# Handing the last gathered column of nine tiles from GpSimd to SyncE, fetched row by row

## The chip, the core and the metric

The kernel runs on one core of a Trainium2 chip. The metric is the device time of one execution in microseconds; the time given is the median of three runs. The change is judged against the time of the kernel before on the same chip.

## What is computed

A recommender's forward pass (DLRM) for 2048 samples, in float32. Each sample has 13 dense features and 26 indices, one into each of 26 tables of 12500 rows of 64 values (256 bytes a row).

```python
h = relu(dense @ dw1 + db1); dense_emb = relu(h @ dw2 + db2)      # (2048, 64)
sparse_emb = emb_tables[f_ids, sparse_idx]                        # (2048, 26, 64)
emb = concatenate([dense_emb[:, None, :], sparse_emb], axis=1)    # (2048, 27, 64)
inter = einsum('bfd,bgd->bfg', emb, emb)
pairs = inter[:, iu0, iu1]                                        # upper triangle, 351
z = concatenate([emb.reshape(2048, -1), pairs], axis=1)
z = relu(z @ ow1 + ob1); z = relu(z @ ow2 + ob2); z = relu(z @ ow3 + ob3)
return z @ ow4 + ob4
```

## The kernel before

The 2048 samples are 16 tiles of 128, a sample to a partition. Each engine has its own program, written out by hand; semaphores join them, and there is no scheduler.

**GpSimd (POOL)** fetches the rows. For each tile `t` it issues 26 indirect DMAs, one for each column `c` (table) of the indices: each brings 128 rows of 256 bytes into `emb[:, t % 4, c // 2, ...]`, 128 partitions at once (L261). The 26 columns are 13 pairs, and the pairs stand in four groups, `GROUPS = [(0, 4), (4, 8), (8, 12), (12, 13)]`: columns 0 to 7, 8 to 15, 16 to 23, and 24 and 25. Each group of each of the four ring places has a semaphore `gathered`. GpSimd's queue has gates (L242 to L260): at column 0, 4, 12, 16, 20 and 24 of a tile it waits until TensorE has got to a given step of this tile or the one before. The gate at column 4 of a tile is "all four groups of the tile before are transposed".

**TensorE (PE)** works through the tile in this order (L819 to L838): transposes of group 0 (L635), the second half of the pair products of the tile before (`gram`, L671), layer 1 of the first features (L683, L692), the pairs of the tile before (L654, L700), transposes of group 1, the turned hidden layer of the tile before (L707), more of layer 1, then transposes of group 2 and of group 3, the rest of layer 1 (ten instructions on the profile's row), and the first half of this tile's `gram`. For every fourth tile or so an upper layer (`upper`, L724, L729, L733) is set in: in tiles 4 to 11 one after the first half of `gram`, in tiles 13 and 14 also ahead of the transposes of group 2 and 3. The last tile, 15, has a finer order of its own (L839 to L869) and ends with the last layers and the store of its results.

**VectorE and ScalarE** evacuate what TensorE leaves in PSUM. VectorE first turns the indices into row numbers (L278, L280, L283), then sets constants, then waits for TensorE's first transposes of group 1.

**SyncE (SP)** issues the loads of weights (L221 to L229), and then only six stores of results `out_dram<-y` (L236), each one run of up to 512 values from one partition, after a wait for the last upper layer of the batch.

Of the kernel before, what the change touches and what calls it, by code (L numbers as in the profile page):

```python
# [6 lines left out]

F32 = mybir.dt.float32
I32 = mybir.dt.int32
U32 = mybir.dt.uint32  # L10
ALU = mybir.AluOpType
ACT = mybir.ActivationFunctionType

P = 128

GROUPS = [(0, 4), (4, 8), (8, 12), (12, 13)]
BATCHES = [(0, 4), (4, 8), (8, 12), (12, 14), (14, 15), (15, 16)]
LAST = BATCHES[-1][0]
LAST_GROUPS = [(0, 4), (4, 8), (8, 10), (10, 12), (12, 13)]


def bass_dlrm_kernel(
    nc: bass.Bass,
    dense_t: bass.AP,
    idx: bass.AP,
    first: bass.AP,
    table: bass.AP,
    dw1: bass.AP,
    dw2: bass.AP,
# [11 lines left out]
    D = dw1.shape[1]  # L41
    H1, H2, H3 = ow1.shape[1], ow2.shape[1], ow3.shape[1]
    TILES = B // P
    NF = idx.shape[2]
    NP = NF // 2
# [8 lines left out]
    RING = 4  # L54
    NG = len(GROUPS)
# [7 lines left out]
    with ExitStack() as ctx:  # L63
        def sb(name, shape, dt=F32):
            return ctx.enter_context(nc.sbuf_tensor(name, shape, dt))

        def psum(name, shape):
            return ctx.enter_context(nc.psum_tensor(name, shape, F32))

        def sem(name):  # L70
            return ctx.enter_context(nc.semaphore(name))

        tr_ps = psum("tr_ps", [P, 2, CHUNK])
        gram_ps = psum("gram_ps", [P, SETS, CHUNK])
        l1_ps = [psum(f"l1_ps{i}", [P, CHUNK]) for i in range(2)]

        first_sb = sb("first_sb", [P, 2, NF], I32)
        idx_raw = sb("idx_raw", [P, TILES, NF], I32)
        wrap = sb("wrap", [P, TILES, NF])
        idx_f = sb("idx_f", [P, TILES, NF])  # L80
        rows = sb("rows", [P, TILES, NF], U32)
        emb = sb("emb", [P, RING, NP, 2 * D])

        feat = [sb(f"feat{i}", [P, NP, P]) for i in range(2)]
        slots = [sb(f"slots{i}", [P, HALF, SETS, QUAD]) for i in range(2)]
# [33 lines left out]
        gathered = [[sem(f"gathered{r}_{n}") for n in range(NG)] for r in range(RING)]  # L119
# [45 lines left out]
        last_l4 = sem("last_l4")  # L165
        last_y = sem("last_y")

        w1_dram = ow1[D:D + NP * P, :].rearrange("(k p) n -> p k n", p=P)

        block = ctx.enter_context(nc.Block())  # L170

        def end_stage(t):

            if 4 <= t < 12:
                return divmod(t - 4, 4)
            return {12: (2, 0), 13: (2, 2), 14: (3, 2)}.get(t)
# [5 lines left out]
        def groups(t):  # L182
            return LAST_GROUPS if t == LAST else GROUPS

        def out_count(stage):
            return 4 * stage[0] + stage[1] + 1
# [25 lines left out]
        def last_turned(c):  # L212

            return (tr_ps[0:PR, 0, 0:P], tr_ps[0:PR, 1, 0:P], l1_ps[0][0:PR, 0:P])[c]

        def upper_cols(b):
            return (BATCHES[b][1] - BATCHES[b][0]) * P

        @block.sync
        def _(sp):  # L220
            sp.dma_start(first_sb[:], first).then_inc(first_in, 16)  # L221
            sp.dma_start(ident_sb[:], ident).then_inc(ident_in, 16)
            sp.dma_start(w1d_sb[:], ow1[0:D, :]).then_inc(w1d_in, 16)
            for n, (a, b) in enumerate(GROUPS):
                sp.dma_start(w1_sb[:, a:b, :], w1_dram[:, a:b, :]).then_inc(w1_in[n], 16)
            sp.dma_start(w1p_sb[:], ow1_pairs.rearrange("(c r) n -> r c n", r=PR)).then_inc(w1p_in, 16)
            sp.dma_start(w2_sb[:], ow2.rearrange("(k p) n -> p k n", p=P)).then_inc(w234_in, 16)
            sp.dma_start(w3_sb[:], ow3.rearrange("(k p) n -> p k n", p=P)).then_inc(w234_in, 16)
            sp.dma_start(w4_sb[:], ow4).then_inc(w234_in, 16)  # L229

            for b, (a, e) in enumerate(BATCHES):
                if a == LAST:
                    sp.wait_ge(last_y, 1)
                else:
                    sp.wait_ge(upper_out, 4 * b + 4)
                sp.dma_start(out[a * P:e * P, :].rearrange("b o -> o b"), y[:, a * P:e * P]).then_inc(out_stored, 16)  # L236
            sp.wait_ge(out_stored, 16 * len(BATCHES))

        @block.gpsimd
        def _(pool):  # L240
            for t in range(TILES):
                pool.wait_ge(rows_in, min(t, 1) + 1)  # L242
                for n, (a, b) in enumerate(GROUPS):
                    if t >= 1:
                        if n == 0:
                            pool.wait_ge(transposed, t * NG - 2)
                            if t >= 2:
                                pool.wait_ge(h1_turned, t - 1)
                        elif n == 2:
                            pool.wait_ge(transposed, t * NG + 1)  # L250
                            pool.wait_ge(gram_done, 2 * t)
                        elif n == 3:
                            pool.wait_ge(transposed, t * NG + 2)
                    for c in range(2 * a, 2 * b):
                        if t >= 1 and c == 4:
                            pool.wait_ge(transposed, t * NG)
                        elif t >= 1 and c == 12:
                            pool.wait_ge(gram_done, 2 * t - 1)
                        elif t >= 1 and c == 20:
                            pool.wait_ge(pairs_turned, t)  # L260
                        pool.indirect_dma_start(  # L261
                            out=emb[:, t % RING, c // 2, c % 2 * D:(c % 2 + 1) * D], out_offset=None, in_=table,
                            in_offset=bass.IndirectOffsetOnAxis(ap=rows[:, t, c:c + 1], axis=0),
                        ).then_inc(last_gathered[(c // 2 - a) // 2] if t == LAST and n == 2 else gathered[t % RING][n], 16)

        @block.vector
        def _(dve):
            step = 0
            for a, b in ((0, 1), (1, TILES)):
                if a == 0:  # L270
                    dve.wait_ge(first_in, 16)
                    r = first_sb[:, 1:2, :]
                else:
                    dve.wait_ge(idx_in, 16)
                    r = idx_raw[:, a:b, :]
                w, f = wrap[:, a:b, :], idx_f[:, a:b, :]
                base = first_sb[:, 0:1, :].to_broadcast([P, b - a, NF])
# [3 lines left out]
                                               op0=ALU.max, op1=ALU.add).then_inc(idx_step, 1)  # L281
                dve.wait_ge(idx_step, step + 2)
                nc.vector.scalar_tensor_tensor(out=rows[:, a:b, :], in0=f, scalar=float(V - 1), in1=base,  # L283
                                               op0=ALU.min, op1=ALU.add).then_inc(rows_in, 1)
                step += 2
            for i in range(2):
                nc.vector.memset(slots[i][:, :, :, SLOTS:QUAD], 0.0).then_inc(consts_in, 1)
                nc.vector.memset(pairs_b[i][:, NPAIR:NPAIR + 1], 1.0).then_inc(consts_in, 1)
                nc.vector.memset(pairs_b[i][:, NPAIR + 1:PC * PR], 0.0).then_inc(consts_in, 1)
            dve.wait_ge(dense_w_in, 4 * 16)  # L290

            def evac_features(t, n):
# [52 lines left out]
            def last_group_slots(n):  # L345
                a, b = groups(LAST)[n]
                dve.wait_ge(transposed, LAST * NG + n + 1)
                src = tr_ps[0:D, n % 2, 0:(b - a) * P].rearrange("p (k c h j) -> p h j c k", k=b - a, h=2, j=HALF)
                for h in range(2):
                    last = nc.vector.tensor_copy(slots[LAST % 2][h * D:(h + 1) * D, :, :, a:b], src[:, h])  # L350
                last.then_inc(slots_dve, 1)
# [258 lines left out]
        def _(pe):  # L610
# [12 lines left out]
            def transposes(t, n):  # L623
                a, b = GROUPS[n]
                if n >= 2:
                    pe.wait_ge((slots_act, slots_dve)[n % 2], 2 * t + 1)
                if n == 1 and t >= 1 and end_stage(t - 1):
                    pe.wait_ge(upper_out, out_count(end_stage(t - 1)))
                if n == 2 and t >= 1:
                    pe.wait_ge(pairs_in, t)  # L630
                if n == 3 and mid_stages(t):
                    pe.wait_ge(upper_out, out_count(mid_stages(t)[0]))
                pe.wait_ge(gathered[t % RING][n], (t // RING + 1) * 32 * (b - a))
                for k in range(a, b):
                    last = nc.tensor.transpose(tr_ps[:, n % 2, (k - a) * P:(k - a + 1) * P], emb[:, t % RING, k, :],  # L635
                                               ident_sb[:])
                last.then_inc(transposed, 1)

            def last_transposes(n):
                a, b = LAST_GROUPS[n]  # L640
                if n in (2, 3):
                    pe.wait_ge(last_gathered[n - 2], 32 * (b - a))
                else:
                    pe.wait_ge(gathered[LAST % RING][3], (LAST // RING + 1) * 32)
                for k in range(a, b):
                    last = nc.tensor.transpose(tr_ps[:, n % 2, (k - a) * P:(k - a + 1) * P], emb[:, LAST % RING, k, :],
                                               ident_sb[:])
                last.then_inc(transposed, 1)
# [287 lines left out]
```

## Time and profile before

| | us |
|---|---|
| median of 3 runs (543.19 to 543.59) | 543.25 |
| the profiled execution | 543.07 |
| its span, first to last instruction | 541.3 |
| TensorE busy with matmuls | 442.5 (82%) |
| GpSimd busy | 392.8 (73%), 416 gathers |
| chain that ended last | POOL 48%, PE 24%, issue 18%, DMA 7% |

The span is what the trace shows; the rest, 1.8 us, lies around it. "Issue" in the chain is time in which an engine waited for nothing that the profile shows; between two gathers of GpSimd it is a constant part of their pitch. A row "idle before <- releaser" says how long the engine stood still ahead of the instruction and what ended that.

### The profile page before, as it was taken

What the parts mean: (1) busy time and instruction counts of PE and PEld (TensorE: products, weight loads), DVE (VectorE), ACT (ScalarE), POOL (GpSimd) and SP (SyncE); (2) the same over time, 40 slices, a digit from 0 to 9 for tenths busy, and PEclk for the clock granted to TensorE, in tenths of its full rate; (3) what the DMA queues carried; (4) which work ended last, traced back from release to release, by engine and by line L of the source; (5) the groups of instructions that cost most, each with busy time, mean ns of one, the idle gap of its engine ahead of it and who ended that gap; (6) DMA issues with size and microseconds to landing.
All of it is one profiled execution on the core that took longest, in us unless ns stands there. A gap on an engine that the chain in (4) does not pass through costs nothing.

```text
span 541.3 us, 5812 instructions
## 1 busy us (share of the span) xinstructions
PE 442.5 (82%) x2262; PEld 235.0 (43%) x2262; DVE 151.4 (28%) x295; ACT 149.0 (28%) x334; POOL 392.8 (73%) x420
## 2 busy tenths in 40 slices
PE   3997879586895969879596997979789598898997
PEld 1245335242533535345253543535344254535686
DVE  1021414132140331414132140432214133241342
ACT  1423124131321422224141231323124141422422
POOL 5777777777777777777777777777777777777750
PEclk9998979799797988989798897999979799999999
DMA  8633323233332333323233232323323233332320
GB/s 265 151 48 28 26 27 28 26 28 27 27 26 27 27 26 28 27 26 28 27 28 27 26 28 26 28 26 29 26 26 28 26 27 26 28 26 26 28 23 2
DMA packets 17168, 19.40 MB, mean 36 GB/s; under 512 B 7359, under 2 KB 8386, under 8 KB 17127
## 3 DMA queue, kind: packets, MB, share of 16 engines
q0 software_dynamic: 13312, 13.66, 30.3%
q1 hardware_dynamic: 3408, 5.02, 2.8%
q10 hardware_dynamic: 420, 0.34, 0.3%
q8 instruction: 18, 0.29, 0.2%
q14 instruction: 10, 0.08, 0.0%
HBM read 18.99 MB, written 0.01 MB: 35 GB/s over the span
## 4 chain that ended last, share of the span: by engine, by line
POOL 48%; PE 24%; issue 18%; DMA 7%; DVE 1%; ACT 1%; POOLq 0%
POOL emb L261 48%; DMA emb<-table_dram,rows 7%; PE l_ps L692 7%; PE gram_ps L671 6%; PE l_ps L700 3%; PE tr_ps L635 2%; PE tr_ps L724 1%; PE l_ps L786 1%; PE gram_ps L786 1%; PE l_ps L683 1%; DVE pairs L310 1%; PE l_ps L707 0%; PE tr_ps L654 0%; ACT h L486 0%; DMA first_sb<-first_dram 0%
## 5 line engine op out<-in xcount | busy, mean ns | idle before, releaser
L261 POOL DMA_INDIRECT emb<-table_dram,rows x416 | 392.6, 944 | 130.1 <-issue 121.0
L692 PE MATMUL l_ps<-w_sb,feat 128*128 128x512 f32 x390 | 200.9, 665 | 0.9 <-DVE feat L296 0.9
L692 PEld LDWEIGHTS l_ps<-w_sb,feat 128*128 128x128 f32 x390 | 80.5, 217 | 101.1 <-issue 98.2
L635 PE MATMUL tr_ps<-ident_sb,emb 128*128 128x128 f32 x203 | 39.7, 315 | 69.8 <-DMA emb<-table_dram,rows 68.5
L329 DVE COPY gram_c<-gram_ps 32x432 f32<-32x432 f32 x60 | 36.5, 609 | 145.5 <-PE gram_ps L671 145.1
L635 PEld LDWEIGHTS tr_ps<-ident_sb,emb 128*128 128x128 f32 x203 | 26.6, 155 | 103.6 <-issue 89.4
L296 DVE COPY feat<-tr_ps 128x512 f32<-128x512 f32 (+2 forms) x33 | 16.1, 489 | 177.6 <-PE tr_ps L635 174.8
L671 PEld LDWEIGHTS gram_ps<-slots 64*128 64x128 f32 x960 | 57.0, 191 | 14.5 <-issue 13.7
L671 PE MATMUL gram_ps<-slots 64*128 64x108 f32 x960 | 62.2, 281 | 0.3 <-DVE gram_c L329 0.3
L469 ACT COPY gram_c<-gram_ps 32x432 f32<-32x432 f32 x60 | 30.5, 508 | 114.1 <-PE gram_ps L671 113.4
L449 ACT COPY feat<-tr_ps 128x512 f32<-128x512 f32 (+1 forms) x32 | 18.5, 577 | 130.5 <-PE tr_ps L635 129.8
L700 PE MATMUL l_ps<-w1p_sb,pairs 118*128 118x512 f32 x90 | 42.6, 610 | 9.8 <-DVE pairs L310 9.8
L457 ACT COPY slots<-tr_ps 64x256 f32<-64x256 f32 (+1 forms) x128 | 50.3, 393 | 1.1
L305 DVE COPY slots<-tr_ps 64x256 f32<-64x256 f32 (+2 forms) x128 | 44.3, 346 | 1.3
L336 DVE STREAM_TRANSPOSE gram_b<-gram_c 128x864 f32<-128x864 f32 x15 | 28.1, 1871 | 0.8
L700 PEld LDWEIGHTS l_ps<-w1p_sb,pairs 118*128 118x128 f32 x90 | 15.9, 190 | 27.8 <-issue 15.3
L486 ACT ACTIVATE h<-l_ps 128x512 f32<-128x512 f32 x15 | 9.0, 597 | 64.1 <-PE l_ps L700 64.1
L724 PE MATMUL tr_ps<-h1t,w_sb 128*128 128x512 f32 x48 | 22.1, 604 | 0.0
L310 DVE COPY pairs<-tr_ps 118x384 f32<-118x384 f32 x15 | 8.4, 557 | 30.0 <-PE tr_ps L654 30.0
L683 PE MATMUL l_ps<-w1d_sb,dense_e 64*128 64x512 f32 x30 | 16.6, 635 | 0.0
L613 PE MATMUL gram_ps<-dense_sb,dw_sb 13*64 13x512 f32 x8 | 7.1, 1063 | 8.9 <-DMA dw_sb<-dw_dram 8.9
L724 PEld LDWEIGHTS tr_ps<-h1t,w_sb 128*128 128x128 f32 x48 | 8.7, 190 | 9.6 <-issue 9.1
(103 smaller groups left out, 197.1 us busy)
## 6 DMA issues: line engine op xcount, KB each, us to landing
emb<-table_dram,rows POOLq DMA_INDIRECT x416, 3.3
w_sb<-ow_dram SPq DMA_DIRECT2D x3, 1024.0 KB, 10.0
w1p_sb<-ow_pairs_dram SPq DMA_DIRECT2D x1, 708.0 KB
w_sb<-ow_dram SPq DMA_DIRECT2D x1, 512.0 KB, 20.9
w_sb<-ow_dram SPq DMA_DIRECT2D x1, 256.0 KB, 12.0
idx_raw<-idx_dram ACTq DMA_DIRECT2D x1, 208.0 KB, 2.6
w1d_sb<-ow_dram SPq DMA_DIRECT2D x1, 128.0 KB, 4.3
w_sb<-ow_dram SPq DMA_DIRECT2D x1, 128.0 KB, 6.4
```

The source lines that it names most:

```text
L261: pool.indirect_dma_start(out=emb[:, t % RING, c // 2, c % 2 * D:(c % 2 + 1) * D], out_offset=None, in_=table, in_offset=bass.IndirectOffs ...
L305: last = nc.vector.tensor_copy(slots[t % 2][h * D:(h + 1) * D, :, :, base:base + b - a], src[:, h])
L329: last = nc.vector.tensor_copy(dst, src)
L336: nc.vector.transpose(gram_b[t % 2][:, 0:SLOTS, :], gram_c[:].rearrange("p i g -> p g i")).then_inc(gram_turned, 1)
L457: last = nc.scalar.copy(slots[t % 2][h * D:(h + 1) * D, :, :, base:base + b - a], src[:, h])
L469: last = nc.scalar.copy(dst, src)
L635: last = nc.tensor.transpose(tr_ps[:, n % 2, (k - a) * P:(k - a + 1) * P], emb[:, t % RING, k, :], ident_sb[:])
L671: mm = nc.tensor.matmul(gram_ps[:, bank, r * GCOLS:(r + 1) * GCOLS], x.rearrange("p c f -> p (c f)"), x[:, :, 0:SLOTS], start=True, stop=True)
L683: nc.tensor.matmul(l1_ps[t % 2][:], dense_e[:, t * P:(t + 1) * P], w1d_sb[:], start=True, stop=False)
L692: nc.tensor.matmul(l1_ps[t % 2][:], feat[t % 2][:, n - 1, :], w1_sb[:, n - 1, :], start=False, stop=False)
L700: mm = nc.tensor.matmul(l1_ps[t % 2][:], pairs[t % 2][:, c, :], w1p_sb[:, c, :], start=False, stop=c == PC - 1)
L724: mm = nc.tensor.matmul(upper_ps(b, s)[:, 0:n], w2_sb[:, k, s * P:(s + 1) * P], h1t[b % 2][:, k, 0:n], start=(k == 0), stop=(k == M1 - 1))
```

## The change

For the nine tiles of `OWN` (2, 4, 5, 7, 8, 10, 12, 13, 14) column 25, the last, is no longer gathered by GpSimd. SyncE fetches its 128 rows one at a time: it loads 32 byte addresses at a time from SBUF into registers, and issues for each a DMA of 256 bytes into one partition of a buffer of its own (`own`, with a place for each of the nine tiles, so no place is used twice). Column 24 of these tiles, which shares the pair with column 25, is gathered by GpSimd into the same buffer. The byte addresses come from four VectorE instructions on one partition of 1152 values (9 x 128), fed by one more load on SyncE's queue. TensorE's group 3 waits in these tiles for one gather fewer and for all 128 fetches. The host only passes the same indices a second time, in another order.

```diff
+OWN = [2, 4, 5, 7, 8, 10, 12, 13, 14]
+HELD = 32
...
+        own = sb("own", [P, len(OWN), 2 * D])
+        own_raw = sb("own_raw", [1, 2, len(OWN) * P], I32)
+        own_f = sb("own_f", [1, 2, len(OWN) * P])
+        own_at = sb("own_at", [1, len(OWN) * P], U32)
...
+        def pair_of(t, k):
+            return own[:, OWN.index(t), :] if t in OWN and k == NP - 1 else emb[:, t % RING, k, :]
+
+        def landed(t, n):
+            a, b = GROUPS[n]
+            return 16 * sum(2 * (b - a) - (n == NG - 1 and s in OWN) for s in range(t % RING, t + 1, RING))
...
                 sp.dma_start(w1_sb[:, a:b, :], w1_dram[:, a:b, :]).then_inc(w1_in[n], 16)
+            sp.dma_start(own_raw[:], own_idx).then_inc(own_in, 16)
             sp.dma_start(w1p_sb[:], ow1_pairs.rearrange("(c r) n -> r c n", r=PR)).then_inc(w1p_in, 16)
...
+            sp.wait_ge(own_rows, 1)
+            held = [sp.alloc_register(f"row{j}") for j in range(HELD)]
+            flat = table.rearrange("r d -> (r d)").bitcast(U8)
+            for i in range(len(OWN)):
+                for q in range(P // HELD):
+                    sp.reg_load(held, own_at[0:1, i * P + q * HELD:i * P + (q + 1) * HELD])
+                    for j in range(HELD):
+                        at = sp.snap(held[j], min_val=0, max_val=(NF * V - 1) * D * 4)
+                        p = q * HELD + j
+                        sp.dma_start(own[p:p + 1, i, D:2 * D].bitcast(U8),
+                                     flat[bass.ds(at, 4 * D)].rearrange("(o d) -> o d", o=1)).then_inc(fetched[i], 16)
...
+                        if t in OWN and c == NF - 1:
+                            continue
                         pool.indirect_dma_start(
-                            out=emb[:, t % RING, c // 2, c % 2 * D:(c % 2 + 1) * D], out_offset=None, in_=table,
+                            out=pair_of(t, c // 2)[:, c % 2 * D:(c % 2 + 1) * D], out_offset=None, in_=table,
...
+            dve.wait_ge(own_in, 16)
+            r, base = own_raw[:, 0, :], own_raw[:, 1, :]
+            w, f = own_f[:, 0, :], own_f[:, 1, :]
+            nc.vector.tensor_scalar(w, r, 0.0, float(V), ALU.is_lt, ALU.mult).then_inc(own_step, 1)
...
+            nc.vector.tensor_scalar(own_at[:], w, float(4 * D), None, ALU.mult).then_inc(own_rows, 1)
             dve.wait_ge(dense_w_in, 4 * 16)
...
-                pe.wait_ge(gathered[t % RING][n], (t // RING + 1) * 32 * (b - a))
+                pe.wait_ge(gathered[t % RING][n], landed(t, n))
+                if t in OWN and n == NG - 1:
+                    pe.wait_ge(fetched[OWN.index(t)], 16 * P)
```

SyncE's program of the kernel before, from the last load of weights for layer 1 to the stores (`w_sb` stands for the weights of several layers):

```order
L226 DMA w1p_sb<-ow_pairs_dram 118x3x512
L227 DMA w_sb<-ow_dram 128x4x256
L228 DMA w_sb<-ow_dram 128x2x128
L229 DMA w_sb<-ow_dram 128x1
L236 DMA out_dram<-y 1x512 x3
```

The same place in the changed kernel. The last two rows come 36 times in all (9 tiles, 4 quarters of 32 rows) ahead of the first store:

```order
L246 DMA own_raw<-own_idx_dram 1x2304
L247 DMA w1p_sb<-ow_pairs_dram 118x3x512
L248 DMA w_sb<-ow_dram 128x4x256
L249 DMA w_sb<-ow_dram 128x2x128
L250 DMA w_sb<-ow_dram 128x1
L257 TENSOR_LOAD own_at
L261 DMA own<-table_dram 1x256 x32
```

One load has come in ahead of `w1p_sb`, and 36 register loads and 1152 fetches stand between the weights and all six stores. Each fetch is two instructions on SyncE: a register move (the copy that `snap` makes, which this listing leaves out) and the DMA.

GpSimd's program of the changed kernel from tile 0 on. The kernel before has in its place the one row `L261 DMA emb<-table_dram,rows 128x64 x416`:

```order
L296 DMA emb<-table_dram,rows 128x64 x76
L296 DMA own<-table_dram,rows 128x64
L296 DMA emb<-table_dram,rows 128x64 x50
L296 DMA own<-table_dram,rows 128x64
L296 DMA emb<-table_dram,rows 128x64 x24
```

After column 23 of tile 2 (76 gathers) comes column 24, into `own`, and then at once column 0 of tile 3; tiles 4 and 5 follow in the same way. In all 407 gathers are left of 416; the gates stay at their columns.

## Rows read from the trace of the kernel before

**Rows 1.** The page: its head, and busy time of each engine.
```profile
span 541.3 us, 5812 instructions
PE 442.5 (82%) x2262; PEld 235.0 (43%) x2262; DVE 151.4 (28%) x295; ACT 149.0 (28%) x334; POOL 392.8 (73%) x420
```

**Rows 2.** The page's costliest groups: count, busy us, mean ns, idle before and its releasers.
```profile
L261 POOL DMA_INDIRECT emb<-table_dram,rows x416 | 392.6, 944 | 130.1 <-issue 121.0
L635 PE MATMUL tr_ps<-ident_sb,emb 128*128 128x128 f32 x203 | 39.7, 315 | 69.8 <-DMA emb<-table_dram,rows 68.5
```

**Rows 3.** Timeline of POOL: tile 6 column 4, tile 14 column 25, tile 15 column 25.
```profile
203.93 0.94 POOL L261 DMA_INDIRECT emb<-table_dram,rows  x1 [0.30 <-issue]
...
489.79 0.95 POOL L261 DMA_INDIRECT emb<-table_dram,rows  x1 [0.30 <-issue]
...
522.24 0.94 POOL L261 DMA_INDIRECT emb<-table_dram,rows  x1 [0.30 <-issue]
```

**Rows 4.** Timeline of PE: transposes of groups 2 and 3 of tile 5, 2 of 6.
```profile
198.59 0.76 PE L635 MATMUL tr_ps<-ident_sb,emb 128*128 128x128 f32 x4 [2.18 <-DMA emb<-table_dram,rows]
201.11 0.45 PE L635 MATMUL tr_ps<-ident_sb,emb 128*128 128x128 f32 x1 [1.76 <-DMA emb<-table_dram,rows]
...
231.15 0.63 PE L635 MATMUL tr_ps<-ident_sb,emb 128*128 128x128 f32 x4 [1.68 <-DMA emb<-table_dram,rows]
```

**Rows 5.** Timeline of PE, tiles 12 to 15: transposes only (the rows between them cut).
```profile
428.35 0.45 PE L635 MATMUL tr_ps<-ident_sb,emb 128*128 128x128 f32 x1 [1.45 <-DMA emb<-table_dram,rows]
...
459.10 0.60 PE L635 MATMUL tr_ps<-ident_sb,emb 128*128 128x128 f32 x4
460.82 0.30 PE L635 MATMUL tr_ps<-ident_sb,emb 128*128 128x128 f32 x1 [1.12 <-DMA emb<-table_dram,rows]
...
470.68 0.65 PE L635 MATMUL tr_ps<-ident_sb,emb 128*128 128x128 f32 x4 [1.38 <-DMA emb<-table_dram,rows]
...
492.04 0.60 PE L635 MATMUL tr_ps<-ident_sb,emb 128*128 128x128 f32 x4
493.20 0.30 PE L635 MATMUL tr_ps<-ident_sb,emb 128*128 128x128 f32 x1 [0.57 <-DMA emb<-table_dram,rows]
...
525.62 0.33 PE L646 MATMUL tr_ps<-ident_sb,emb 128*128 128x128 f32 x1
```

**Rows 6.** Timeline of SyncE's queue: start us, us of issuing, line.
```profile
0.75 0.41 SPq L221 DMA_DIRECT2D first_sb<-first_dram  x1
1.21 0.41 SPq L222 DMA_DIRECT2D ident_sb<-ident_dram  x1
...
5.47 0.37 SPq L226 DMA_DIRECT2D w1p_sb<-ow_pairs_dram  x1
5.89 16.15 SPq L227 DMA_DIRECT2D w_sb<-ow_dram  x1
...
25.02 2.21 SPq L229 DMA_DIRECT2D w_sb<-ow_dram  x1
```

**Rows 7.** Source L236, the stores: ns min/median/max of issuing, first and last start.
```profile
L236 SPq DMA_DIRECT2D out_dram<-y x6: 227/228/282, 276.7 to 539.8; - x6
```

**Rows 8.** DMA, 276 to 280 us: SyncE's queue (packets, MB, share) and its store.
```profile
q1 hardware_dynamic: 2, 0.00, 0.1%
out_dram<-y SPq DMA_DIRECT2D x1, 2.0 KB
```

**Rows 9.** Source L221, the first load: from issue to landing.
```profile
DMA to landing us min/median/max: 2.4/2.4/2.4
```

**Rows 10.** Timeline of DVE: two of the index steps, and its first evacuation.
```profile
3.71 0.35 DVE L278 TENSOR_SCALAR wrap<-idx_raw 128x390 f32<-128x390 int32 x1
...
4.71 0.57 DVE L283 SCALAR_TENSOR_TENSOR rows<-idx_f,first_sb 128x390 uint32<-128x390 f32 x1
...
33.57 0.69 DVE L296 COPY feat<-tr_ps 128x512 f32<-128x512 f32 x1 [27.57 <-PE tr_ps L635]
```

**Rows 11.** Tile emb, POOL: a gather's ns min/median/max, first and last start.
```profile
L261 POOL DMA_INDIRECT emb<-table_dram,rows x416: 940/944/1075, 4.1 to 522.2; - x139
```

More of the change, by code:

```diff
@@ L9 @@
 I32 = mybir.dt.int32
+U8 = mybir.dt.uint8
 U32 = mybir.dt.uint32
@@ L26, in bass_dlrm_kernel @@
     first: bass.AP,
+    own_idx: bass.AP,
     table: bass.AP,
@@ L166, in bass_dlrm_kernel @@
         last_y = sem("last_y")
+        own_in = sem("own_in")
+        own_step = sem("own_step")
+        own_rows = sem("own_rows")
+        fetched = [sem(f"fetched{i}") for i in range(len(OWN))]
         w1_dram = ow1[D:D + NP * P, :].rearrange("(k p) n -> p k n", p=P)
@@ L289, in _ @@
                 nc.vector.memset(pairs_b[i][:, NPAIR + 1:PC * PR], 0.0).then_inc(consts_in, 1)
+            dve.wait_ge(own_in, 16)
+            r, base = own_raw[:, 0, :], own_raw[:, 1, :]
+            w, f = own_f[:, 0, :], own_f[:, 1, :]
+            nc.vector.tensor_scalar(w, r, 0.0, float(V), ALU.is_lt, ALU.mult).then_inc(own_step, 1)
+            dve.wait_ge(own_step, 1)
+            nc.vector.scalar_tensor_tensor(out=f, in0=r, scalar=float(-V), in1=w,
+                                           op0=ALU.max, op1=ALU.add).then_inc(own_step, 1)
+            dve.wait_ge(own_step, 2)
+            nc.vector.scalar_tensor_tensor(out=w, in0=f, scalar=float(V - 1), in1=base,
+                                           op0=ALU.min, op1=ALU.add).then_inc(own_step, 1)
+            dve.wait_ge(own_step, 3)
+            nc.vector.tensor_scalar(own_at[:], w, float(4 * D), None, ALU.mult).then_inc(own_rows, 1)
             dve.wait_ge(dense_w_in, 4 * 16)
@@ L632, in transposes @@
                     pe.wait_ge(upper_out, out_count(mid_stages(t)[0]))
-                pe.wait_ge(gathered[t % RING][n], (t // RING + 1) * 32 * (b - a))
+                pe.wait_ge(gathered[t % RING][n], landed(t, n))
+                if t in OWN and n == NG - 1:
+                    pe.wait_ge(fetched[OWN.index(t)], 16 * P)
                 for k in range(a, b):
-                    last = nc.tensor.transpose(tr_ps[:, n % 2, (k - a) * P:(k - a + 1) * P], emb[:, t % RING, k, :],
+                    last = nc.tensor.transpose(tr_ps[:, n % 2, (k - a) * P:(k - a + 1) * P], pair_of(t, k),
                                                ident_sb[:])
@@ L643, in last_transposes @@
                 else:
-                    pe.wait_ge(gathered[LAST % RING][3], (LAST // RING + 1) * 32)
+                    pe.wait_ge(gathered[LAST % RING][3], landed(LAST, NG - 1))
                 for k in range(a, b):
@@ L916 @@
         "first_dram": _np.stack([base, idx[:, 0]], axis=1),
+        "own_idx_dram": _np.stack([_np.concatenate([idx[:, t, NF - 1] for t in OWN]),
+                                   _np.full(len(OWN) * P, (NF - 1) * V, _np.int32)])[None].astype(_np.int32),
         "table_dram": x["emb_tables"].reshape(NF * V, D),
```

## The prediction

> **What bounds the kernel now.** I read the page's busy times first [rows 1]: TensorE has 82%, GpSimd 73%, so neither is plainly the bound. The groups settle it [rows 2]: the 416 gathers take 0.944 us each and stand apart by "issue", and TensorE's transposes waited 68.5 us for gathered rows. From the last gather's start, 522.24, back to tile 14's last, 489.79, there are 26 steps [rows 3]: 1.248 us a gather. From the first start, 4.1 [rows 11], 415 such steps lead to 522.0, so GpSimd never stood at a gate for long: it paces the kernel. The timeline of TensorE says how closely it follows. Ahead of groups 2 and 3 of tile 5 it waited 2.18 and 1.76 us, ahead of group 2 of tile 6 1.68 [rows 4]; from one group 3 to the next group 2 it works 231.15 - 1.68 - 201.11 = 28.4 us without waiting, against 24 gathers (columns 0 to 23) of 30.0. Tiles 12 to 15 have more upper layers [rows 5]. From 470.68 on TensorE waits for rows once, 0.57 us at 493.20, and never again until the end.
>
> **What GpSimd gives.** Nine gathers less are 9 x 1.248 = 11.24 us. In a tile of `OWN` group 3 waits for column 24, and column 0 of the next tile starts one step after it, so every distance from group 3 to a later gate is as before, and so is the 30.0 us to the next group 2 that TensorE's 28.4 must fit into. The gather of tile 14's column 25 started at 489.79 and TensorE went on at 493.20: 3.4 us from start to use.
>
> The gain does not reach the end whole. I follow TensorE from tile 12's group 3 [rows 5]. Six columns are dropped ahead of tile 12, and there column 24 counts instead of 25: 428.35 - 7 x 1.248 = 419.61. TensorE then works without a wait for rows until 459.70 (the end of group 2 of tile 13), 31.35 us, so it reaches group 3 at 450.96; the rows are there at 460.82 - 8 x 1.248 = 450.83. Group 0 of tile 14 is bound by its gathers, 8 steps earlier: 460.69. TensorE's 21.96 us from there to the end of group 2 of tile 14 (492.64) lead to 482.65; column 24 has landed at 493.20 - 11.24 = 481.96. So group 3 of tile 14 starts at 482.65 instead of 493.20, 10.55 us earlier, and the 48.1 us behind it are TensorE's own work: the last transposes at 525.62 came only when the last gather (522.24 + 3.4) did, and those move by 11.24. **The full gain is 10.55 us**, if SyncE is in time.
>
> **What SyncE must do.** 1152 fetches, 36 register loads. It is free at 25.02 + 2.21 = 27.2 us [rows 6]. The addresses should be ready by then: their load stands ahead of `w1p_sb`, behind which the next issue was held until 22.0 [rows 6], and the four VectorE steps, scaled from 390 to 1152 values in proportion, are at most 2 x 0.35 x 2.95 + 2 x 0.57 x 2.95 = 5.4 us [rows 10]. That could end at 27.4 at the latest; VectorE is not wanted before 33.57. Start: 27.3. A landing takes 2.4 us [rows 9].
>
> With c the time for one fetch, the i-th column has landed at 29.7 + 128 c i. Group 3 is wanted at 4.2 + 3.4 + 1.248 for each gather ahead of column 24, so at 102.5 for tile 2 (76 gathers ahead), then at 166.1, 197.3, 261.0, 292.2 and 355.8 for tiles 4, 5, 7, 8 and 10; for tiles 12, 13 and 14 it is 419.6, 450.96 and 482.65, from above. So c may be 0.569, 0.533, 0.436, 0.452, 0.410, 0.425, 0.435, 0.411 and **0.393**: tile 14 decides. Past that, group 3 of tile 14 starts at 29.7 + 1152 c. At 493.20, c = **0.402**, the whole gain is gone. A fetch lasting a hundredth of a microsecond longer costs 11.5 us, and the stores queued behind the fetches cost nothing as long as these end before the last store.
>
> **What one fetch costs.** No row shows one. The nearest is SyncE's store of a single run from one partition: 0.228 us to issue [rows 7]. Two packets went out for it, the data and the count [rows 8], so it ran on one DMA engine, and a fetch has its shape, one run of 256 bytes. Between two issues lie 1.21 - 0.75 - 0.41 = 0.05 us [rows 6]; a fetch has two instructions, move and DMA, so 0.10. The register load is bounded by nothing below; above, if it is one read of SBUF, by a whole DMA's way of 2.4 us, for 32 fetches 0.075 each. I take the middle, 0.04. That an address comes from a register can cost nothing more, or the issue can be as long as that of a 128-partition load, 0.41 [rows 6]. Ends: 0.228 + 0.05 = 0.28 with a free move and a free load, and 0.41 + 0.10 + 0.075 = 0.59. Value: 0.228 + 0.10 + 0.04 = **0.37**, near the lower end because the shape is the store's. Then SyncE ends at 27.3 + 1152 x 0.37 + 2.4 = 456, 27 us before TensorE wants it, and the margin is 0.02 us a fetch.
>
> One rule of the Trainium skill would make this otherwise. The page "DMA: Bandwidth & Descriptors", section "Why a DMA increments its semaphore by 16 and not by 1", says that a copy is spread over the largest number of engines up to 16 that divides its slowest dimension, and a contiguous run of 256 would by it go to 16. By that rule the store of 512 values would have been spread too; the trace shows two packets, and disagrees, so I do not count on it. Were it so, the issue would be the 0.41 of the upper end.
>
> **Small terms.** The fetches carry 1152 x 256 bytes, 0.3 MB, beside 416 x 128 x 256 bytes, 13.6 MB, of gathers, so they take little from the DMA engines; were a gather to land some tenths later for it, that would cost once and not in each tile, since GpSimd's pitch doesn't wait for landings. The load of `own_raw` lies in SyncE's hold at L227. TensorE's extra wait on `fetched` is one more check of a semaphore, nine times, inside its waits for rows except at tiles 13 and 14; I take it at nothing.
>
> **Sum.** 541.3 - 10.55 = 530.75 us of span. The profiled execution had 1.8 us around its span, and stands 0.2 under the median: 530.75 + 1.8 + 0.2 = 532.7 for the median.
>
> **The rivals.**
> First, SyncE is slightly late: c from 0.393 to 0.402. The time is 543.25 - (493.20 - 29.7 - 1152 c): at 0.398, 538.2. My c lies only 0.02 below this stretch. Chance 0.08 on the faster side, and 0.03 within 0.2%, that is 1.1 us, about what a measurement of this kernel can tell (c from 0.4014 to 0.4033).
>
> Second, on the other side, SyncE is the new bound: from c = 0.4033 the kernel is slower. The whole kernel then stands at tile 14's group 3 and, since GpSimd's gate at column 4 needs group 3, GpSimd too, once a column is later than 203.93 - 201.56 = 2.4 us [rows 3, 4]. For it: what I left out needs only 0.03 us a fetch, from the register load, the address or the issue. Against it: the shape's own row is 0.228. At 0.41 the time is 552.1, at 0.44 586.6, and at 0.59 543.25 + 29.7 + 679.7 - 493.2 = 759. A form of it is a register load that fetches its 32 values one by one: if one value cost as much as an issue, 0.228, c would be 0.56 and the time 725; no row speaks for or against it. Chance of the form 0.08, of this rival in all 0.27.
> The Trainium skill has such a rule: "Runtime: NRT & Kernel Launch", section "Instruction fetch mechanics", gives about 200 ns for each register even in bulk, for loads from HBM. As an estimate by it c would be 0.53 and the time some 690. No run here shows whether a load from SBUF goes by it.
>
> Third, GpSimd does not keep its pitch: its 407 gathers become slower beside 1152 more DMAs. 11.24 / 407 = 0.028 us a gather, 3%, would eat all. Against it: over the whole execution, the first 27 us with all the weights' loads among it, a gather's instruction took 940 to 1075 ns, with the median at 944 [rows 11]. Chance 0.02 of slower.
>
> **How the numbers follow.** Full gain, 532.7: 0.60, own range 531 to 534.5. Late but faster 0.08, the same 0.03, slower 0.29, of which I put 0.09 up to 560 (c = 0.417) and the rest beyond. Faster is 0.60 + 0.08 = 0.68. The range from 530.8 to 560 holds 0.60 + 0.08 + 0.03 + 0.09 = 0.80.
>
> **What would show it.** SyncE's queue: its first fetch at about 27.3 and the pitch of the fetches, 0.37, decides everything; the last at about 454. GpSimd's last gather at 522.24 - 11.24 = 511.0, with pitch 1.248. TensorE's group 3 of tile 14 at 482.65 without a wait, in tiles of `OWN` its wait ahead of group 3 shorter by 1.25, to about 0.5, and none released by the fetches. I am wrong if group 3's releaser is a DMA into `own` from SyncE and GpSimd shows pauses at column 4 of tiles 3, 5, 6, 8 and so on.

## The result: 12.9% slower

| | before | changed |
|---|---|---|
| median of 4 runs, us | 543.41 | 612.91 (611.59 to 616.24) |
| ratio | | 1.1288, 95% interval 1.1273 to 1.1304 |
| span of the profiled execution, us | 541.3 | 611.1 |

The forecast was 532.7 us.

The page of the changed kernel, in its parts on queues, chain and groups (those groups that answer to [rows 2]):

```profile
PEclk9997888989899599979757989897979859955999
...
SPq 71%; issue 20%; PE 7%; DVE 1%; ACT 0%; DMA 0%
SPq L261 48%; SPq L257 12%; SPq L259 6%; SPq L248 3%; PE l_ps L741 1%; PE l_ps L835 1%; PE gram_ps L835 1%; PE gram_ps L720 1%; SPq L250 1%; SPq L245 1%; PE l_ps L749 0%; SPq L249 0%; DVE gram_c L376 0%; PE l_ps L842 0%; PE gram_ps L842 0%
...
L296 POOL DMA_INDIRECT emb<-table_dram,rows x398 | 376.2, 945 | 200.8 <-issue 115.8
L684 PE MATMUL tr_ps<-ident_sb,own 128*128 128x128 f32 x9 | 3.6, 400 | 80.7 <-DMA own<-table_dram 80.7
```

The chain no longer goes through GpSimd but through SyncE's queue (SPq, 71%): L261 is the fetch, L257 the register load, L259 the move that `snap` makes. TensorE waited 80.7 us for `own`. Its timeline shows where, of the nine group 3 only those that waited:

```profile
206.59 0.45 PE L684 MATMUL tr_ps<-ident_sb,own 128*128 128x128 f32 x1 [9.04 <-DMA own<-table_dram]
...
324.68 0.45 PE L684 MATMUL tr_ps<-ident_sb,own 128*128 128x128 f32 x1 [25.18 <-DMA own<-table_dram]
...
501.74 0.45 PE L684 MATMUL tr_ps<-ident_sb,own 128*128 128x128 f32 x1 [19.49 <-DMA own<-table_dram]
```

These are tiles 5, 8 and 13. Tile 14, the fourth, waited 26.9 us, until 560.80; in the other five tiles of `OWN` the fetches were in time. SyncE's two lines, by source, tell why (ns of one, minimum, median, maximum):

```profile
L257 SPq TENSOR_LOAD <-own_at x36: 2027/2120/2218, 28.1 to 545.3; - x36
...
L261 SPq MOVE own<-table_dram x1152: 29/29/38, 30.2 to 559.4; - x192
L261 SPq DMA_DIRECT2D own<-table_dram x1152: 224/225/325, 30.3 to 559.5; - x192
```

From the first load, 28.1, to the last fetch, 559.5, are 531.4 us for 1152 fetches: **0.461 us each**. Each went out as two packets on SyncE's queue (5714 packets for 3408 in the kernel before, of which the 1152 fetches make 2304). The last was in use 1.3 us later, at 560.80, and 50.3 us of TensorE's work follow: 611.1.

A late fetch stops GpSimd too. Its timeline at tile 9, column 4, ahead of which it must see group 3 of tile 8:

```profile
301.20 0.94 POOL L296 DMA_INDIRECT emb<-table_dram,rows  x1 [0.30 <-issue]
325.40 0.94 POOL L296 DMA_INDIRECT emb<-table_dram,rows  x1 [23.25 <-PE tr_ps L684]
```

The other pauses over 2 us stand at column 4 of tiles 6, 14 and 15, each behind a late tile.

### The profile page after: what moved, and what is told of

It reads as the page before. It is cut to its first block, busy times and chain, and to the rows that moved or that the text cites. A ratio compares the mean times of both kernels' runs of the same rounds, so it can differ in the third digit from the quotient of the medians.

```text
span 611.1 us, 9304 instructions
## 1 busy us (share of the span) xinstructions
PE 448.0 (73%) x2262; PEld 238.8 (39%) x2262; DVE 155.6 (25%) x299; ACT 148.9 (24%) x334; POOL 384.9 (63%) x411
## 3 DMA queue, kind: packets, MB, share of 16 engines
q1 hardware_dynamic: 5714, 5.33, 2.7%
## 4 chain that ended last, share of the span: by engine, by line
SPq 71%; issue 20%; PE 7%; DVE 1%; ACT 0%; DMA 0%
SPq L261 48%; SPq L257 12%; SPq L259 6%; SPq L248 3%; PE l_ps L741 1%; PE l_ps L835 1%; PE gram_ps L835 1%; PE gram_ps L720 1%; SPq L250 1%; SPq L245 1%; PE l_ps L749 0%; SPq L249 0%; DVE gram_c L376 0%; PE l_ps L842 0%; PE gram_ps L842 0%
## 5 line engine op out<-in xcount | busy, mean ns | idle before, releaser
L296 POOL DMA_INDIRECT emb<-table_dram,rows x398 | 376.2, 945 | 200.8 <-issue 115.8
L741 PE MATMUL l_ps<-w_sb,feat 128*128 128x512 f32 x390 | 206.2, 679 | 3.4 <-ACT feat L496 2.5
L741 PEld LDWEIGHTS l_ps<-w_sb,feat 128*128 128x128 f32 x390 | 81.8, 220 | 108.3 <-issue 101.4
L684 PE MATMUL tr_ps<-ident_sb,emb 128*128 128x128 f32 x194 | 34.9, 304 | 50.0 <-DMA emb<-table_dram,rows 49.0
L720 PEld LDWEIGHTS gram_ps<-slots 64*128 64x128 f32 x960 | 58.8, 196 | 15.3 <-issue 13.7
L720 PE MATMUL gram_ps<-slots 64*128 64x108 f32 x960 | 64.1, 286 | 0.8 <-DVE gram_c L376 0.8
L684 PE MATMUL tr_ps<-ident_sb,own 128*128 128x128 f32 x9 | 3.6, 400 | 80.7 <-DMA own<-table_dram 80.7
L684 PEld LDWEIGHTS tr_ps<-ident_sb,emb 128*128 128x128 f32 x194 | 24.9, 152 | 79.8 <-issue 67.6
L504 ACT COPY slots<-tr_ps 64x256 f32<-64x256 f32 (+1 forms) x128 | 50.3, 393 | 1.1
L684 PEld LDWEIGHTS tr_ps<-ident_sb,own 128*128 128x128 f32 x9 | 1.7, 188 | 81.7 <-issue 81.7
L749 PEld LDWEIGHTS l_ps<-w1p_sb,pairs 118*128 118x128 f32 x90 | 15.9, 190 | 27.8 <-issue 15.3
## 6 DMA issues: line engine op xcount, KB each, us to landing
w_sb<-ow_dram SPq DMA_DIRECT2D x1, 512.0 KB, 19.9
```

Source lines behind the costliest of these rows:

```text
L296: pool.indirect_dma_start(out=pair_of(t, c // 2)[:, c % 2 * D:(c % 2 + 1) * D], out_offset=None, in_=table, in_offset=bass.IndirectOffsetO ...
L504: last = nc.scalar.copy(slots[t % 2][h * D:(h + 1) * D, :, :, base:base + b - a], src[:, h])
L720: mm = nc.tensor.matmul(gram_ps[:, bank, r * GCOLS:(r + 1) * GCOLS], x.rearrange("p c f -> p (c f)"), x[:, :, 0:SLOTS], start=True, stop=True)
L741: nc.tensor.matmul(l1_ps[t % 2][:], feat[t % 2][:, n - 1, :], w1_sb[:, n - 1, :], start=False, stop=False)
L749: mm = nc.tensor.matmul(l1_ps[t % 2][:], pairs[t % 2][:, c, :], w1p_sb[:, c, :], start=False, stop=c == PC - 1)
```

## The experiments

Theory A: SyncE's own instructions set the pace of the fetches, and the last one sets the end. Rival B: the small transfers hold SyncE back. Rival C: they slow GpSimd's gathers. The first four kernels ran on one chip, beside a kernel before of 543.98 us (median of 7).

**Addresses written into the program** (no loads, no moves; other rows are fetched than the indices name):

```diff
-                    sp.reg_load(held, own_at[0:1, i * P + q * HELD:i * P + (q + 1) * HELD])
-                        at = sp.snap(held[j], min_val=0, max_val=(NF * V - 1) * D * 4)
+                        at = ((NF - 1) * V + (i * P + q * HELD + j) * 10) * D * 4
```

> The nine columns are fetched from rows known when the program is written: no register loads and no moves, still 1152 DMAs of 256 bytes from SyncE (the rows fetched are not those the indices name). Theory A, SyncE's own instructions set the pace (0.225 us to issue, 0.16 for moves and steps between instructions, 0.07 for the register load): the pitch falls to 0.225 + 0.04 = 0.27 us, the last fetch is issued at about 28 + 311 = 339 us, no tile waits for it, and the time is that of the full gain, 532 to 533.5 us. Rival B, the small transfers themselves hold SyncE back (a full queue, one DMA engine): the pitch stays above 0.38 and the time above 590 us. Rival C, 1152 more DMAs slow GpSimd's gathers: pitch of the fetches falls, but GpSimd's rises above 1.248 and the time stays above 536 us.

Measured: 534.64 us, ratio 0.9831 (0.9815 to 0.9848). The fetch by its source, then TensorE's transposes of groups 2 and 3 of tile 14:

```profile
L260 SPq DMA_DIRECT2D own<-table_dram x1152: 219/247/537, 27.2 to 366.8; - x192
```
```profile
483.06 0.60 PE L683 MATMUL tr_ps<-ident_sb,emb 128*128 128x128 f32 x4
483.50 0.27 PE L683 MATMUL tr_ps<-ident_sb,own 128*128 128x128 f32 x1
484.33 4.56 PE L740 MATMUL l_ps<-w_sb,feat 128*128 128x512 f32 x10 [0.57 <-ACT feat L495]
```

The pitch is (366.8 - 27.2) / 1151 = 0.295 us, so 1152 transfers of the same size go through in two thirds of the time: B falls. I had expected 0.27 and at most 533.5 us, both a little too low. C falls by the gathers: from the fifteenth (22.64 us; 21.68 in the kernel before) to the last (512.02; 522.24) there are 392 and 401 steps, and both come to 1.248 us with and without fetches beside them. And the other half of the prediction is seen alone: group 3 of tile 14 at 483.50, where 482.65 was forecast.

**One move less** (fresh registers for each load, their values used without a copy):

```diff
-            held = [sp.alloc_register(f"row{j}") for j in range(HELD)]
...
+                    held = [sp.alloc_register(f"row{i}_{q}_{j}") for j in range(HELD)]
                     sp.reg_load(held, own_at[0:1, i * P + q * HELD:i * P + (q + 1) * HELD])
-                        at = sp.snap(held[j], min_val=0, max_val=(NF * V - 1) * D * 4)
+                        at = sp.snap(held[j], donate=True, min_val=0, max_val=(NF * V - 1) * D * 4)
```

> Fresh registers for every load, whose values are used without a copy: one of the two moves of a fetch is gone, all else as in the change. Theory A: the pitch inside a quarter falls from 0.384 by 0.034 + 0.022 to 0.328, with loads 0.40 a fetch; the last fetch of tile 14 is in at 28.1 + 461 to 465 + 1.3 = 490 to 494 us, where the kernel before had its group 3 at 493.2: 540 to 545 us, no change within one per cent. Theory B: the pitch doesn't fall, 613 us.

Measured: 534.59 us, ratio 0.9832 (0.9815 to 0.9848): better than expected, by a little that decides. This is the change's whole computation, and it is faster than the kernel before; the gain is small, but its interval lies clear of 1. By source:

```profile
L261 SPq DMA_DIRECT2D own<-table_dram x1152: 224/225/326, 30.0 to 481.9; - x192
...
L257 SPq TENSOR_LOAD <-own_at x36: 2086/2124/2264, 27.8 to 469.7; - x36
```

(481.9 - 27.8) / 1152 = 0.394 us a fetch instead of 0.461, with the rows that the indices name, so B falls here too. One move of 0.034 us is gone, and with it 0.067: its steps to its neighbours count as much as the move. GpSimd keeps 1.248 us beside fetches that now run until 481.9. The last fetch went out at 481.9, 1.3 us to its use is 483.2, and TensorE got there at 483.84. My expectation had 490 to 494; the last columns were in time by 0.6 us.

**Seven columns**, for the tiles that stand behind the end of their fetches at the measured pace:

```diff
-OWN = [2, 4, 5, 7, 8, 10, 12, 13, 14]
+OWN = [2, 4, 6, 8, 10, 11, 13]
```

> Only seven columns, for tiles 2, 4, 6, 8, 10, 11 and 13, each of which stands behind the moment at which its fetches end at 59.05 us a column (89, 148, 207, 266, 325, 384, 443 us). Theory A with the prediction's account of GpSimd and TensorE: nothing waits for a fetch, 7 x 1.248 = 8.7 us are gained, 534.5 us. If GpSimd's or TensorE's side of the account is wrong (a gate, a slower pitch beside the fetches), it stays above 538 us.

Measured: 536.07 us, ratio 0.9862 (0.9845 to 0.9878), no wait for `own`. The span is 533.5, 7.8 us less, where 8.7 were expected; in ratio to its own kernel before 7.9 us.

**Registers loaded 8 at a time** (`HELD = 8`, 144 loads):

> Registers are loaded 8 at a time, 144 loads instead of 36. Theory A1, a load costs by the register (2.12 us / 32 = 0.066 each): a load of 8 takes 0.53 us, the pitch over all stays 0.46 and the time near 613 us. Theory A2, a load costs 2.1 us whatever its size: 0.384 + 0.265 = 0.65 us a fetch, the last in at 780 us, the time about 830 us.

Measured: 656.1 us (a single run, so without an interval). Neither form fits:

```profile
L257 SPq TENSOR_LOAD <-own_at x144: 688/782/963, 26.7 to 600.4; - x144
```

8 registers take 0.782 us and 32 take 2.120. A straight line through these two sizes has (2.120 - 0.782) / 24 = 0.056 us a register and 0.34 a load. So, as an estimate, more than 32 registers at a time would still save little; the price is mostly by the register. The last fetch went out at 604.0 us, so the 1152 fetches took 604.0 - 26.7 = 577.3 us, 45.9 more than in the changed kernel. The loads themselves explain 144 x 0.782 - 36 x 2.120 = 36.3 of it; the rest lies in the steps around 108 more loads and in other steps. So the loads' time stands in full in the pace of the fetches.

The other fourteen runs were made on four other chips, where the kernel before itself took 640 to 648 us instead of 544, so their times say nothing on the questions put to them. They are of four programs and a variant:

| | time, us | kernel before there |
|---|---|---|
| e5, f5, g2: fetches beside all 416 gathers | 699.93, 702.99, 713.15 | 639.93, 643.13, 648.06 |
| e6, f6, g1, h1: one register load in all | 800.18, 796.77, 801.32, 795.99 | 639.93, 643.13, 648.06, 640.61 |
| e7, f7, h3: the change without tile 14 | 817.59, 817.53, 809.91 | 639.93, 643.13, 640.61 |
| e8, f8 and g3, h2: one move less, addresses on 36 partitions | 728.69, 735.63, 736.98, 733.11 | 639.93, 643.13, 648.06, 640.61 |

The last is in two forms: in g3 and h2 the indices are also loaded second on SyncE's queue.

Fetches beside all gathers, three times:

> GpSimd gathers all 416 columns as before and TensorE reads them; SyncE makes its 1152 fetches with one move each beside it, into a buffer that nobody reads. What is left is the price of the fetches for the others. Theory A: GpSimd keeps its pitch of 1.249 us while they run, and only the four VectorE steps at 16 to 20 us hold it, 0.5 to 0.9 us in all: 0.5 to 1 us over the kernel before, 544.5 to 545 us where that is 544. Rival C, the small transfers slow the gathers: each tenth of a per cent of pitch is 0.5 us; above 546 us it would be shown.

> The kernel of e5_fetch_only once more, beside a kernel before that takes its usual 544 us (in that call it took 640). GpSimd gathers all 416 columns and TensorE reads them; SyncE makes its 1152 fetches with one move each into a buffer that nobody reads. Theory A: GpSimd keeps its pitch of 1.249 us while they run and only the four VectorE steps at 16 to 20 us hold it: 0.5 to 1 us over the kernel before, 544.5 to 545. Rival C, the small transfers slow the gathers: above 546 us.

> GpSimd gathers all 416 columns and TensorE reads them; SyncE makes its 1152 fetches with one move each beside it, into a buffer that nobody reads. Theory A: GpSimd keeps its pitch of 1.249 us while they run, and only the four VectorE steps at 16 to 20 us hold it: 0.5 to 1 us over the kernel before. Rival C, the small transfers slow the gathers: 2 us or more over it.

One register load, four times (`sp.reg_load` under `if i + q == 0:`):

> The change with a single register load instead of 36: both moves stay, the same 32 rows are fetched for every quarter (so the rows are not those of the indices). Theory A: 0.384 us inside a quarter plus 0.01 for the boundaries of instruction fetch, 0.393 in all; the last fetch is in at 28 + 453 + 1.3 = 482 us, as TensorE gets there, and the time is that of the full gain, 534.6 us. The load term alone, 1152 x 0.067 = 77 us, then separates 613 from 535. If something else holds the fetches, the time stays above 560 us.

> The kernel of e6_load_once once more, for the same reason: a single register load instead of 36, both moves stay, the same 32 rows are fetched for every quarter (so the rows are not those of the indices). Theory A: 0.393 us a fetch in all, the last in at 28 + 453 + 1.3 = 482 us as TensorE gets there, 534.6 us; if something else holds the fetches, above 560 us.

> The change with a single register load instead of 36: both moves stay, the same 32 rows are fetched for every quarter (so the rows are not those of the indices). Theory A: 0.393 us a fetch in all, the last in at 28 + 453 + 1.3 = 482 us as TensorE gets there, 534.6 us where the kernel before takes 544; if something else holds the fetches, above 560 us.

> The change with a single register load instead of 36; both moves stay, the same 32 rows are fetched for every quarter (so the rows are not those of the indices). Theory A: 0.393 us a fetch in all, the last in at 482 us as TensorE gets there, 0.983 of the kernel before (534.6 us where it takes 544); if something else holds the fetches, above 560 us.

Without tile 14 (`OWN = [2, 4, 5, 7, 8, 10, 12, 13]`), three times:

> The change without tile 14: eight columns at 59.05 us. The last is in at 501.7 us for tile 13, whose group 3 was at 460.8 before. If the last late column sets the end and GpSimd restarts from its gate at column 4 behind it, group 3 of tile 14 follows 8.5 + 22 us behind at 532.2, and the end 48 to 50 us behind that: span 580.5 to 583, time 582.5 to 585 us. If the lateness of a column simply adds up over the late tiles, the time is 543.5 + 9.0 + 25.2 + 19.5 - 10.0 = 587 us or more.

> The kernel of e7_eight once more: the change without tile 14. If the last late column sets the end and GpSimd restarts from its gate at column 4 behind it: 582.5 to 585 us. If the lateness of the columns adds up: 587 us or more.

> The change without tile 14: eight columns at 59.05 us. If the last late column sets the end and GpSimd restarts from its gate at column 4 behind it: 582.5 to 585 us. If the lateness of the columns adds up: 587 us or more.

One move less and 36 partitions, in both forms:

> Nine columns with one move a fetch (as e2_donate9); the addresses worked out on 36 partitions of 32 values instead of one of 1152, and the load of the pair weights moved to ScalarE's queue, so that SyncE is not held behind it. Theory A: the four VectorE steps take 0.2 us instead of 0.75 to 1.35 and no longer hold GpSimd (0.5 us back), SyncE starts its fetches near 18 us instead of 28, and the last is in at 473 us, ten ahead of TensorE. 534.0 us where e2_donate9 had 534.6; no more, since TensorE is the bound of the end.

> The kernel of e8_best once more: nine columns with one move a fetch, the addresses worked out on 36 partitions, the load of the pair weights on ScalarE's queue. SyncE starts its fetches near 25 us, as in that call, and they end some 2 to 3 us earlier than in e2_donate9; GpSimd is not held at 16 to 20 us. 534.0 us where e2_donate9 had 534.6, and no less, since TensorE is the bound of the end.

> Nine columns with one move a fetch; the addresses worked out on 36 partitions, their indices loaded second on SyncE's queue, the load of the pair weights on ScalarE's queue. SyncE starts its fetches near 18 us instead of 30 and ends them near 470, twelve before TensorE needs the last; the VectorE steps take 0.2 us each and GpSimd is no longer held at 16 to 20 us. 0.5 us below e2_donate9 (0.983 of the kernel before): 0.982; no less, since TensorE is the bound of the end.

> Nine columns with one move a fetch; the addresses worked out on 36 partitions, their indices loaded second on SyncE's queue, the load of the pair weights on ScalarE's queue. SyncE starts its fetches near 21 us instead of 30 and ends them near 472; GpSimd's first 15 gathers take 17.6 us as in the kernel before and not 18.1. 0.5 us below e2_donate9: 0.982 of the kernel before; no less, since TensorE is the bound of the end.

In their traces SyncE's instructions, moves as well as DMAs, again and again take 0.7 or 1.4 us. The median of the fetch stays 225 ns, but the mean pitch in h2 is (671.8 - 19.9) / 1152 = 0.57 us. By source, h2:

```profile
L260 SPq DMA_DIRECT2D own<-table_dram x1152: 2/225/1395, 22.1 to 671.8; - x192
```

The cause stays open; no run told it. All fourteen took 1.09 to 1.28 times the kernel before there (e5 1.085, e6 1.240, e8 1.139). None of these programs ran where the kernel before takes 544 us, so how much of that is the place and how much the program isn't shown. So three things stay untried where they could be told: what taking the loads away alone gives back (77 us by the trace of the changed kernel, borne out in part by the run with 8 registers), how late columns add up, and what the version of g3 is worth.

One piece can be used, since it ends before 21 us and has its counterpart in the same kind of trace: the VectorE steps. In the changed kernel, VectorE and GpSimd:

```profile
16.22 0.92 DVE L328 TENSOR_SCALAR own_f<-own_raw 1x1152 f32<-1x1152 int32 x1 [10.06 <-DMA own_raw<-own_idx_dram]
17.17 1.35 DVE L330 SCALAR_TENSOR_TENSOR own_f<-own_raw,own_f 1x1152 f32<-1x1152 int32 x1
```
```profile
15.62 0.94 POOL L296 DMA_INDIRECT emb<-table_dram,rows  x1 [0.30 <-issue]
16.86 1.09 POOL L296 DMA_INDIRECT emb<-table_dram,rows  x1 [0.30 <-issue]
18.26 1.08 POOL L296 DMA_INDIRECT emb<-table_dram,rows  x1 [0.30 <-issue]
19.64 1.17 POOL L296 DMA_INDIRECT emb<-table_dram,rows  x1 [0.30 <-issue]
```

Three gathers take 1.08 to 1.17 us instead of 0.94 while VectorE works on one partition: 0.5 us, once (0.9 in e1, where a fourth took 1.48). One partition need not be the reason: in the kernel before, the first gather, beside the index steps on 128 partitions, took 1.07. In h2 the same steps run on 36 partitions and are over at 7.2:

```profile
6.59 0.18 DVE L329 SCALAR_TENSOR_TENSOR own_f<-own_raw,own_f 36x32 f32<-36x32 int32 x1
```
```profile
17.18 0.94 POOL L295 DMA_INDIRECT emb<-table_dram,rows  x1 [0.30 <-issue]
18.43 0.95 POOL L295 DMA_INDIRECT emb<-table_dram,rows  x1 [0.30 <-issue]
```

Its first 14 steps take 17.6 us, as in the kernel before and as expected of h2, against 18.1 in e2 and 18.5 in e1.

## Why the prediction was wrong

The forecast was a gain, and the kernel lost 12.9%. The step that failed is **what one fetch costs**, 0.37 us; it was 0.461. Put into the prediction's own formula, 29.7 + 1152 x 0.461 = 560.8 us, where group 3 of tile 14 started at 560.80. Term by term:

| term | predicted | measured |
|---|---|---|
| issue of the DMA | 0.228 | 0.225 |
| moves and steps between instructions | 0.10 | 0.159 |
| register load | 0.04 | (2.536 - 0.384) / 32 = 0.067 |
| rest (one longer step in 128 instructions) | 0 | 0.010 |
| sum | 0.37 | 0.461 |

From one fetch to the next are 0.384 us inside a quarter, and 2.536 from a quarter's last fetch over the load to the next one (medians of the starts in the trace). So 0.384 - 0.225 = 0.159 is left for the second row, and the load adds 2.152 us for 32 fetches. What I had taken was one move, without a duration, only two steps of 0.05. A fetch is three instructions on SyncE, not the two that I had counted when I described the change. There are two moves: the copy that `snap` makes (L259) and one that the DMA itself brings for its register address (L261, 29 ns), which the listing of the program doesn't show. The address in a register cost the issue nothing (0.225 against 0.247 with written addresses) but brought this move. The register load was taken as one read; it goes by the register. The last row is a step about 0.3 us longer every 42 or 43 fetches. In the trace these steps lie 128 SyncE instructions apart, with three instructions to a fetch here, with two in e2 (every 63 fetches) and with one in e1; why isn't shown.

The sum lies inside its bounds (0.28 to 0.59), and so does the load (0.067 under 0.075). But the moves do not: 0.159 us, where even the upper end had only 0.10. The issue fell at its lower end and hid that. This term is the largest part of the miss, 0.059 of 0.09, the load 0.027 and the longer steps 0.010. The sum came out 0.06 beyond the edge at 0.402 that I had worked out.

**What bounds the kernel; what GpSimd gives**: right. The pitch of 1.248 held, and where fetches were in time (e1) GpSimd's last gather started at 512.02, forecast 511.0. The third rival did not come.

**TensorE's part of the gain**: right in kind, 0.9 us too large. Group 3 of tile 14 came at 483.50 (e1) and 483.84 (e2) for 482.65, and 48.1 us followed in e1, so the span fell by 9.7 instead of 10.55. Two things had been taken at nothing. The VectorE steps hold GpSimd by 0.5 us, in e1 by 0.9, and in e1 that alone is about the difference, since group 0 of tile 14 was still bound by its gathers there (it waited 0.71 us for rows, and began at 461.70). And TensorE's 31.35 us from tile 12's group 3 on were not the same again: in e2 the stretch up to tile 13's group 3 took 33.78 us at a granted clock of 0.91, against 0.96 in the kernel before, with 0.46 us idle ahead of group 3 that no wait for rows explains (e1 has them too, at a clock of 0.95 and 32.49 us; in the kernel before, the wait for rows stood in that place). So in e2 TensorE, and not the gathers, came late to tile 14. Why the granted clock differs isn't shown. The windows of the kernel before and of e2:

```profile
428.35:460.82 32.47, 30.34 (x134) 15.50 (x135) 9.88 (x18) 8.64 (x20) 24.53 (x26) 0.96 0.33 27
```
```profile
419.73:453.51 33.78, 31.86 (x135) 15.83 (x135) 9.86 (x18) 9.39 (x21) 25.54 (x28) 0.91 0.33 28
```

The columns are the stretch, its us, busy us of TensorE, its weight loads, VectorE, ScalarE and GpSimd, the granted clock, DMA share and GB/s.

**SyncE's start and the landing**: the load went out at 28.1 for 27.3; issue to use was 1.3 us for 2.4. They nearly cancel, by luck: 29.4 for 29.7.

**The second rival** is what happened, with its place and its gate: at its c of 0.44 it gave 586.6, and at 0.461 its formula gives 610.8. The form in which values are fetched one by one had the right mechanism and a price four times too high. Its nearest companion, the Trainium skill's page "Runtime: NRT & Kernel Launch", section "Instruction fetch mechanics", has about 200 ns a register for loads from HBM; here, from SBUF, the traces have 0.056 us a register and 0.34 a load. **The first rival**, slightly late, has its place in e2, which was in time by 0.6 us. The spread over 16 engines did not show either: two packets a fetch, and the issue stayed at 0.225. The prediction had read that rule wrongly. The Trainium skill's page "DMA: Bandwidth & Descriptors", section "Why a DMA increments its semaphore by 16 and not by 1", counts the dimensions as the instruction carries them, and in the trace the store and the fetch each stand as one element (of 2048 and of 256 bytes). So the page and the trace agree.

The tail was 50.3 us and not 48.1. Behind the 27 us of idling ahead of 560.8, in which the granted clock had gone down to 0.56 on the mean (533 to 560.8 us), the granted clock of TensorE was 0.94 in this stretch (0.99 in the kernel before). The window of the changed kernel:

```profile
560.80:611.10 50.30, 45.37 (x482) 34.70 (x482) 16.04 (x36) 13.83 (x37) 20.77 (x22) 0.94 0.19 16
```

## What to carry to other kernels

Where a cost is repeated a thousand times, the edge at which it decides (here 0.40 us) is to be worked out first; if the estimate lies within the width of its unknown terms, chances should be near even, however near the closest row seems. Count every instruction the issuing engine runs for a step, with the time to its neighbour, since here, where SyncE does nothing else, leaving out a move of 34 ns gave back 67. And the work can be cut to the pace: one move less in a fetch turned 12.9% slower into 1.7% faster, and two columns less into 1.4% faster.

## What the runs showed that I had not expected

A register load from SBUF costs about 0.34 us and 0.056 a register (0.782 us for 8, 2.120 for 32).

SyncE made a step some 0.3 us longer every 128 instructions of its own, whatever they were: about 10 us over the 1152 fetches.

A gather's issue on GpSimd took 1.08 to 1.17 us instead of 0.94 beside plain VectorE instructions of 0.75 to 1.35 us. The Trainium skill, "DMA: Bandwidth & Descriptors", section "SWDGE vs HWDGE vs iDMA", says that GpSimd writes its descriptors into SBUF, that VectorE locks it out there while it runs in its 2-port mode, and that the DMAs of SyncE are free of this. The traces agree in direction: GpSimd's issues were held by 0.14 to 0.23 us (once 0.54), and SyncE's stayed at 0.225 us, at most 0.325, though VectorE was busy for 155.6 us of the span. Whether these VectorE steps ran in that mode no run here shows.

Last, e2 and the version with addresses on 36 partitions are near relatives. The first took 0.983 of the kernel before; the second took 1.13 to 1.15 of it, where SyncE's instructions took 0.7 us again and again. It seems that a kernel whose path runs through many small instructions of one sequencer suffers most from that, but no program ran in both places except the kernel before.
